# Splitting q and k into three bf16 parts: through PSUM by ScalarE and TensorE in place of VectorE and GpSimd

## The reference

```python
xn = ln(x, ln1_w, ln1_b)                       # after an adaLN norm of x
q = (xn @ q_w + q_b).reshape(B, L, 16, 8)      # 16 heads of 8
k = (xn @ k_w + k_b).reshape(B, L, 16, 8)
v = (xn @ v_w + v_b).reshape(B, L, 16, 8)
attn = softmax(where(causal, q @ k.T * 8 ** -0.5, -inf))
attn_out = (attn @ v) @ o_w + o_b
ssm_out = mamba(xn)                            # conv, silu, a scan over 512 tokens with 16 states
x = x + alpha * attn_out + (1 - alpha) * ssm_out
x = x + gelu(ln(x) @ ffn_w1 + ffn_b1) @ ffn_w2 + ffn_b2
```

## Time and profile before

| what | us |
|---|---|
| median of 3 runs | 1723.49 |
| lowest and highest of them | 1720.03, 1725.16 |
| the profiled execution, its own time | 1718.54 |
| its span from first to last instruction | 1716.3 |
| mean granted TensorE clock, share of full | 0.941 |

### The profile page before, as it was taken

The page is one execution under the profiler, slowest core; times in us unless marked ns, Lnnn a source line. Parts: engine busy times, 40 slices in busy tenths (PEclk is TensorE's granted clock), DMA queues, the critical chain, the costliest instruction groups (busy, mean ns, idle before and its releaser), DMA issues. The chain is left out here.

```text
span 1716.3 us, 22019 instructions
## 1 busy us (share of the span) xinstructions
PE 1425.8 (83%) x7164; PEld 895.0 (52%) x7196; DVE 1336.1 (78%) x2025; ACT 1063.5 (62%) x1776; POOL 848.3 (49%) x866
## 2 busy tenths in 40 slices
PE   4777787887878788797777788799999999968787
PEld 3334444444444344444433655588787777725663
DVE  2359989999898999989961867787677777757856
ACT  2565667586756658576646665687877878722017
POOL 3254768676675777767733312112222222338843
PEclk9878999999999999999989899899999999968889
DMA  3112212222121222212101210011111111000001
GB/s 87 52 48 75 69 59 79 62 70 84 32 88 57 77 70 81 68 42 82 57 1 37 68 53 25 28 38 47 36 47 43 44 46 41 32 0 1 0 1 49
DMA packets 61654, 84.72 MB, mean 49 GB/s; under 512 B 6588, under 2 KB 32038, under 8 KB 61542
## 3 DMA queue, kind: packets, MB, share of 16 engines
q1 hardware_dynamic: 61442, 83.30, 15.5%
q10 hardware_dynamic: 100, 0.03, 0.0%
HBM read 74.38 MB, written 8.78 MB: 48 GB/s over the span
## 5 line engine op out<-in xcount | busy, mean ns | idle before, releaser
L1743 POOL TENSOR_TENSOR dBx<-dtx,Bb 128x512 f32<-128x512 f32 x256 | 320.7, 1275 | 11.4 <-DMA Bb<-b_dram 9.0
L1350 DVE TENSOR_TENSOR hl<-lsq,hh 128x512 fp32r<-128x512 f32 x320 | 260.0, 822 | 84.4 <-ACT hh L1627 76.7
L1317 DVE TENSOR_TENSOR_SCAN hy<-bank,dBx 128x512 f32<-128x512 f32 x256 | 297.9, 1204 | 4.8 <-POOL dBx L1743 4.8
L1035 PE MATMUL bank<-QK 127*128 127x384 bf16 (+6 forms) x992 | 226.1, 309 | 86.6 <-DVE Mx L1301 62.8
L1624 ACT ACTIVATE lsq<-bank,vcol 128x512 f32<-128x512 f32 x320 | 219.5, 693 | 105.2 <-DVE hl L1350 62.7
L1564 ACT ACTIVATE PT<-bank 128x512 f32<-128x512 f32 x320 | 184.5, 595 | 110.9 <-PE bank L1035 66.9
L1762 POOL TENSOR_TENSOR stage<-stage,lrs 128x512 f32<-128x512 f32 x64 | 93.0, 1453 | 309.8 <-DVE lrs L1430 309.8
L1301 DVE TENSOR_REDUCE Mx<-bank 128x1 f32<-128x384 f32 (+3 forms) x352 | 214.0, 627 | 16.4 <-PE bank L1035 16.0
L1035 PE MATMUL bank<-x,we1h 128*128 128x512 f32 x640 | 210.8, 411 | 18.3 <-ACT hh L1627 9.8
L1611 ACT ACTIVATE bank<-dtv,alog 128x512 f32<-128x512 f32 x256 | 171.5, 692 | 80.5 <-DVE hy L1317 79.5
L1723 POOL TENSOR_SCALAR_AFFINE_SELECT PT<-PT 128x256 f32<-128x256 f32 (+1 forms) x320 | 118.4, 378 | 201.4 <-ACT PT L1564 201.0
(11 more groups left out here) (255 smaller groups left out, 2436.8 us busy)
## 6 DMA issues: line engine op xcount, KB each, us to landing
Bb<-b_dram SPq DMA_DIRECT2D x128, 256.0 KB, 3.8
stage<-w_rows SPq DMA_DIRECT2D x64, 256.0 KB, 3.1
parts<-part SPq DMA_DIRECT2D x16, 384.0 KB, 2.8
QK<-parts SPq DMA_DIRECT2D x64, 96.0 KB
QK<-parts SPq DMA_DIRECT2D x64, 64.0 KB
stage<-in_L_ffn_We_dram SPq DMA_DIRECT2D x16, 256.0 KB, 3.5
hy<-in_L_attn_x_dram SPq DMA_DIRECT2D x8, 256.0 KB, 5.7
QK<-parts SPq DMA_DIRECT2D x64, 32.0 KB
```

Of the source, the lines that this page charges most:

```text
L1035: return engine.matmul(o, l, r, start=start, stop=stop, tile_position=pos, skip_group_check=True)
L1317: engine.tensor_tensor_scan(hst[:, 2 * (g % 3) + h, :], bank[4 + h][:], dBx[:, g % 4, h, :], 0.0, ALU.mult, ALU.add).then_inc(sems["dve_sc ...
L1350: engine.tensor_tensor(hl[:, sl, :], full[:, f, :], hh[:, sl, :].bitcast(F32), ALU.subtract).then_inc(sems["dve_hl"], 1)
L1743: engine.tensor_tensor(dBx[:, sl, h], dtx[:, b % 2, h], Bb[:, sl], ALU.mult).then_inc(sems["pool_dbx"], 1)
```

## The change

The split no longer goes through `qf`. TensorE leaves the product in its bank; ScalarE rounds bank plus bias to bf16 part c; TensorE multiplies part c by minus the identity and accumulates it into the same bank; this for c = 0, 1, 2, with two such subtractions. The scale of q goes into its weights, so that the bank holds what is to be split. VectorE and GpSimd have nothing to do in it any more. For this the bank is taken out of the ring until part 2 has been read, ScalarE's first rounding (not VectorE's) waits for the landing of the parts written before, and TensorE's subtractions wait for ScalarE. The buffer `qf` goes, a bf16 matrix `identn` comes.

```diff
-WORK = dict(pe_max=45, pe_sc=30, pe_ht=45, pe_av=200, pe_qk=95, pe_val=95, pe_mrow=45, pe_dn=95, pe_wo=190, pe_bx=350, pe_dbc=180, pe_dt=95,
-            pe_yt=45, pe_so=190, pe_lnc=95, pe_lnv=95, dve_max=62, dve_scan=113, dve_y=40, dve_ha=70, dve_hs=70, dve_yd=70, dve_qk=50,
+WORK = dict(pe_max=45, pe_sc=30, pe_ht=45, pe_av=200, pe_qk=45, pe_val=95, pe_mrow=45, pe_dn=95, pe_wo=190, pe_bx=350, pe_dbc=180, pe_dt=95,
+            pe_yt=45, pe_so=190, pe_lnc=95, pe_lnv=95, dve_max=62, dve_scan=113, dve_y=40, dve_ha=70, dve_hs=70, dve_yd=70, act_qk=62,
...
     def project(b):
         for i in range(2):
             k = take()
-            it = step("qk0", b=b, i=i, bank=k, free=free.get(f"b{k}"), ready=r_n[b], qf=free.get("qf"), part=free.get("part"))
-            it["m"], it["q"], it["h"] = up("pe_qk"), up("act_qf"), up("dve_qk")
-            free[f"b{k}"] = it["q"]
-            h1 = it["h"]
-            yield
-            it = step("qk1", b=b, i=i, h1=h1, part=free.get("part"))
-            it["m1"], it["h2"] = up("dve_qk"), up("dve_qk")
-            h2 = it["h2"]
-            yield
-            it = step("qk2", b=b, i=i, h2=h2, part=free.get("part"), pd=free.get(f"pd{b % 2}"))
-            it["h3"] = free["qf"] = up("pool_qk")
-            it["d"] = free["part"] = r_parts[b] = up(f"parts_{b % 2}", 16)
-            yield
+            ring.remove(k)
+            last = free.get(f"b{k}"), r_n[b]
+            for c in range(3):
+                it = step("qk", b=b, i=i, c=c, bank=k, ready=last, part=free.get("part"), pd=free.get(f"pd{b % 2}"))
+                it["m"] = up("pe_qk")
+                it["x"] = last = up("act_qk")
+                if c == 2:
+                    it["d"] = free["part"] = r_parts[b] = up(f"parts_{b % 2}", 16)
+                    free[f"b{k}"] = last
+                    ring.append(k)
+                yield
...
-                elif kind == "qk0":
-                    q.wait_ge(("pool_set", pool_set["qk3"]), it["free"], it["ready"])
-                    mm(o[:], wqk[:, it["i"], :], nT[:, it["b"], :]).then_inc(sems["pe_qk"], 1)
+                elif kind == "qk":
+                    q.wait_ge(("pool_set", pool_set["idn"]), it["ready"])
+                    if it["c"] == 0:
+                        mm(o[:], wqk[:, it["i"], :], nT[:, it["b"], :], stop=False).then_inc(sems["pe_qk"], 1)
+                    else:
+                        mm(o[:], identn[:], part[:, it["c"] - 1, :], start=False, stop=it["c"] == 2).then_inc(sems["pe_qk"], 1)
...
-                elif kind == "qk0":
-                    q.wait_ge(it["q"], it["part"])
-                    engine.tensor_copy(part[:, 0, :], qf[:]).then_inc(sems["dve_qk"], 1)
-                elif kind == "qk1":
-                    q.wait_ge(it["h1"])
-                    engine.tensor_tensor(qf[:], qf[:], part[:, 0, :], ALU.subtract).then_inc(sems["dve_qk"], 1)
-                    q.wait_ge(it["m1"], it["part"])
-                    engine.tensor_copy(part[:, 1, :], qf[:]).then_inc(sems["dve_qk"], 1)
...
-                elif kind == "qk0":
-                    q.wait_ge(("dve_set", dve_set["qbs"]), it["m"], it["qf"])
-                    engine.activation(qf[:], o[:], ACT.Identity, scale=QS if it["i"] == 0 else 1.0,
-                                      bias=qbs[:, 0:1] if it["i"] == 0 else col("k_b")).then_inc(sems["act_qf"], 1)
+                elif kind == "qk":
+                    q.wait_ge(("dve_set", dve_set["qbs"]), it["m"], it["part"])
+                    engine.activation(part[:, it["c"], :], o[:], ACT.Identity,
+                                      bias=qbs[:, 0:1] if it["i"] == 0 else col("k_b")).then_inc(sems["act_qk"], 1)
...
-                elif kind == "qk2":
-                    q.wait_ge(it["h2"], it["part"])
-                    engine.tensor_tensor(part[:, 2, :], qf[:], part[:, 1, :], ALU.subtract).then_inc(sems["pool_qk"], 1)
...
-                if kind == "qk2":
+                if kind == "qk" and it["c"] == 2:
                     s = it["b"] % 2
-                    q.wait_ge(it["h3"], it["pd"])
+                    q.wait_ge(it["x"], it["pd"])
```

More of the change, by code:

```diff
@@ L898, in build @@
             mrow = small[32:40].bitcast(BF16).rearrange("p (s t) -> p s t", s=2)
-            qf = tmp("qf", [P, T])
+            identn = tmp("identn", [P, P], BF16)
             part = tmp("part", [P, 3, T], BF16)
@@ L986, in on_set @@
             return {name: i + 1 for i, name in enumerate(names.split())}
-        pool_set = on_set("vrow qk0 qk1 qk2 qk3 wo id0 id om cm on ep mask0 mask idb sel0 sel bsum vb0 mr vb qz0 qz1 qz2")
+        pool_set = on_set("vrow qk0 qk1 qk2 qk3 wo id0 id om cm on ep mask0 mask idb idn sel0 sel bsum vb0 mr vb qz0 qz1 qz2")
         dve_set = on_set("row0 row1 sc0 sc1 neg abs sgn2 max sgn gate om1 av2 av3 A qbs")
@@ L1676, in gpsimd_program @@
                 for f in range(2):
-                    engine.tensor_copy(wqk[:, i, 64 * f:64 * f + 64].rearrange("c (q a) -> c q a", a=4),
-                                       wqk0[:, i, 64 * f:64 * f + 64].rearrange("c (a q) -> c q a", a=4)).then_inc(sems["pool_set"], 1)
+                    engine.tensor_scalar(wqk[:, i, 64 * f:64 * f + 64].rearrange("c (q a) -> c q a", a=4),
+                                         wqk0[:, i, 64 * f:64 * f + 64].rearrange("c (a q) -> c q a", a=4), QS if i == 0 else 1.0, None,
+                                         ALU.mult).then_inc(sems["pool_set"], 1)
             engine.memset(wo[:], 0.0).then_inc(sems["pool_set"], 1)
@@ L1693, in gpsimd_program @@
             engine.tensor_copy(identb[:], ident[:]).then_inc(sems["pool_set"], 1)
+            engine.tensor_scalar(identn[:], ident[:], -1.0, None, ALU.mult).then_inc(sems["pool_set"], 1)
             engine.memset(seld[:], 0.0).then_inc(sems["pool_set"], 1)
```

## The result

| what | us |
|---|---|
| before, median of 12 runs beside the change | 1719.55 |
| the change, median of 12 runs (lowest, highest) | 1726.38 (1723.35, 1731.10) |
| ratio, 95% interval | 1.0033 [1.0020, 1.0047], so +5.7 us [+3.4, +8.1] |
| profiled execution of the change: own time, span | 1725.62, 1723.9 |
| its mean granted TensorE clock | 0.928 (before: 0.941) |

The change is slower by about as much as a measurement of this kernel can tell from nothing. The twelve runs of before hold the three of the first table; the ratio leaves out one disturbed run among them (1786.89; experiment J has one of its own, 2062.12, left out likewise). The change's median lies 2.4 us above the forecast of 1724.0 and within its range. Part of that closeness is luck: the forecast was built on the median of three runs, 1723.49, and twelve runs of the same kernel gave 1719.55.

What follows compares the result with a forecast made beforehand. VectorE bounds the mixers overall, but TensorE and ScalarE were taken to set the projections' time. Summed: 5.1 - 4.6 + 6 x 0.0 = +0.5 us, so 1719.0 profiled, 1724.0 as median; range 1712 to 1736.

Steps and rivals of the forecast that it cites:

- Batch 0, +5.1: Serial stretch before the first scan: round trips between TensorE and ScalarE delay the norms, 5.1 us lost, nothing regained.
- Batch 1, -4.6: After the first scan VectorE has no idle time, so its removed split work is all gained: 4.6 us, at worst 2.3.
- The set-up, 0: Before the batches: one more instruction on GpSimd, which is ahead, costs 0.
- Batches 2 to 7, 0.0 each: Six projections: gains and added work end in the scan starting when it did, 0.0 each, bounds -0.9 and +1.2.
- 1.0 us of slack: Last projection: decay ready at about 764.5, scan takes it at 765.55; the additions, +1.0, use this up.
- the first rival: Batches 2 to 7: VectorE's relief counts, 2.9 us gained in each of six, median 1706.6; chance 0.15 with its larger case.
- the 15.9 us of waiting: VectorE's idle time before six roundings in the mixers, waiting for ScalarE; claimed not to be gained.
- 1.3 us at the start: Start of each unit in batches 2 to 7: VectorE's rounding at 724.76 goes; -0.5 counted, -1.3 as bound.
- the second rival: Batches 2 to 7: the held bank leaves four in the ring, VectorE waits for Mx; sum +9, median 1732.4; chance 0.25.
- 0.4 + 1.8: Each of batches 2 to 7: two TensorE subtractions of q, +0.4, and three added ScalarE roundings, +1.8 us.
- a wait of the scan for the decay: Sign: VectorE's scan newly waits 1 to 2 us for ScalarE's decay once per odd unit; without it the first rival holds.
- the number of waits in front of `Mx`: Sign: Mx waiting for TensorE in many more than 25 places would point to the second rival.

Runs made afterwards that it cites:

- J: Kernel before with changed set-up; batches 2 to 7 make only ScalarE's first rounding, bank held out of the ring for three steps; median 1714.53 us, ratio 0.9978.
- B: The change with batch 0 split the old way, batches 1 to 7 the new; median 1722.22 us, ratio 0.9996 to the kernel before.
- C: Kernel before with the changed set-up and batch 1 alone split the new way; median 1719.48 us, ratio 0.9984.
- G: The change with batch 0's split run beside the norms that follow, one step per norm, in bank 3; median 1718.70 us, ratio 0.9993 to the kernel before.
- K: Kernel before with changed set-up, batch 1 alone split the new way, batch 0's old split run beside the norms; median 1715.83 us, ratio 0.9984.
- A: Kernel before with only the change's set-up (scaled wqk, identn), all eight batches split the old way; median 1721.61 us, ratio 0.9995.
- I: Kernel before with changed set-up; batches 2 to 7 make only ScalarE's first rounding, bank given back at once, parts 1 and 2 left out; median 1701.27 us, ratio 0.9898.
- F: Kernel before with VectorE's subtraction and second rounding left out in batches 2 to 7 (part 1 not written); median 1716.70 us, ratio 0.9982.
- D: Kernel before with the changed set-up and batches 2 to 7 alone split the new way; median 1722.03 us, ratio 0.9999.
- E: Kernel before, old split, but each projection bank kept out of the ring until GpSimd's subtraction; median 1734.24 us, ratio 1.0092.
- M: Kernel before with batch 0's split beside the norms, and GpSimd making VectorE's subtraction and second rounding in batches 2 to 7; median 1711.14 us, ratio 0.9938.

## Why the prediction was right, and where it was not

**Batch 0, +5.1: right.** ScalarE's timeline of the changed kernel, and the first of TensorE's two rows for q:

```profile
54.26 0.69 ACT L1546 ACTIVATE part<-bank,qbs 128x512 bf16<-128x512 f32 x1 [3.50 <-PE bank L1033]
55.64 0.69 ACT L1546 ACTIVATE part<-bank,qbs 128x512 bf16<-128x512 f32 x1 [0.70 <-PE bank L1033]
57.03 0.69 ACT L1546 ACTIVATE part<-bank,qbs 128x512 bf16<-128x512 f32 x1 [0.70 <-PE bank L1033]
60.37 0.69 ACT L1546 ACTIVATE part<-bank,vcol 128x512 bf16<-128x512 f32 x1 [2.65 <-DMA parts<-part]
...
63.14 0.69 ACT L1546 ACTIVATE part<-bank,vcol 128x512 bf16<-128x512 f32 x1 [0.70 <-PE bank L1033]
```

```profile
55.00 0.61 PE L1033 MATMUL bank<-part,identn 128*128 128x512 bf16 x1 [0.84 <-ACT part L1546]
```

A round trip takes 1.38 and 1.39 us, in the range of 1.25 to 1.45; the wait for the landing is the 2.65 forecast. From q's first reading to the table load of batch 0's silu it is 49.78 us (54.26 to 104.04) against 44.46 (52.74 to 97.20): +5.3. By the ratios (the change against B) it is +6.4, 3.8 either way. The first scan stands at 123.37, 7.3 us later and not 5; 1.5 of that the first reading of q was late already. The granted clock is 0.50 in this stretch, the 1.2 GHz level, and the product takes 0.61. The 0.1 that the prediction put down for the product's weights does not show (1.38 is 0.69 and 0.61 and 0.08), which keeps the trip below 1.45 on the slow clock. Of the two figures of the Trainium skill (TensorE: Matmul & The Clock Gate, section Single matmul latency) the measured 0.61 is exactly the one for the slow clock.

**Batch 1, -4.6: right at first, then partly taken back.** Measured from the first scan, the scans of the change stand at -2.70, -3.51 and -4.57 behind the three places of the earlier trace rows (the scans of 121.60, 135.15 and 146.19 before): VectorE's rows were worth their whole length. The prediction stopped there. At the scan of 155.58 it is -3.87, and -3.63 at 163.30, since the freed VectorE meets TensorE in its convolutions. And in B, C and G more went. The convolution in the changed kernel and in B, with the row of VectorE's wait in B:

```profile
146.88 3.69 PE L1033 MATMUL bank<-nT,wtap 128*128 128x512 f32 x8 [1.61 <-DVE Mx L1294]
```

```profile
142.04 6.68 PE L1057 MATMUL bank<-nT,wtap 128*128 128x512 f32 x8 [1.61 <-DVE Mx L1329]
...
149.03 0.69 DVE L1329 TENSOR_REDUCE Mx<-bank 128x1 f32<-128x512 f32 x1 [2.64 <-PE bank L1057]
```

The same eight products took 3.69 and 6.68 us (4.76 in the trace before, 5.41 in C, 6.69 in G). In B the granted clock was 0.50 from 136 to 146 us; TensorE had waited for VectorE there for 2.28 us at 137.05 and for 1.61 us just ahead of the convolution. The change had nearly the same waits (1.89 us at 141.89, then 1.61) and was back at 1.00 when its convolution began; why B was not stays open. At the scan of 163.30 B had kept 0.6 of its 4.6 us, C 1.9 and G 0.6, the change 3.6 and K 3.6. The prediction let a gain come back only through a decay that is held up; it came back through TensorE.

**The set-up, 0: not refuted.** Most traces say 1 to 3 us at the first reading of q, K's and the medians nothing (A). The step named the one instruction added and overlooked that the four scaled copies stand ahead of ident, for which TensorE waits.

**Batches 2 to 7, 0.0 each: the sum right by luck, the steps wrong.** The prediction let five of VectorE's six instructions lie "inside the time that TensorE and ScalarE set", and put the scan of 765.55 behind a decay with 1.0 us of slack. I and F show otherwise. VectorE's relief is worth 2.8 us in each of the six (16.7/6, known to 0.6), where the first rival had 2.9; only the 15.9 us of waiting stayed, as the prediction said. Where k's part of it comes through can be read in the last projection. On TensorE before, the scores ahead of dt's second product waited for an `Mx` that stood behind VectorE's work on k:

```profile
758.53 0.39 PE L1035 MATMUL bank<-QK 128*128 128x384 bf16 x2 [0.51 <-DVE Mx L1301]
```

ScalarE then waited 0.46 us for that product. In F neither waits, and there stand:

```profile
755.89 1.29 ACT L1614 ACTIVATE bank<-dtv,alog 128x512 f32<-128x512 f32 x2
...
756.69 2.33 DVE L1320 TENSOR_TENSOR_SCAN hy<-bank,dBx 128x512 f32<-128x512 f32 x2
```

The scans ahead of VectorE's work on k come 7.38 us earlier than before, this decay 7.95 (it stood at 763.84) and this scan 8.86. So the decay itself moved by 0.57, and the other 0.9 of the 1.48 is the slack that the prediction had kept for the additions.

The prediction's own list holds most of this. Its 1.3 us at the start, the 0.7 of waits that are swallowed and the slack of 1.0 make 3.0 for each batch, close to the 2.8 measured; its words about the five instructions, and the argument against the first rival, leave it out. Wrong in size were the two prices. The held bank takes 13.8 us, 2.3 for each batch; the main sum had let it take 0.8 of the 1.3 at the start of a unit, and the second rival had +9 in all. The roundings and subtractions take 3.6, 0.6 for each (1.1 by the scans), where the sum had 0.4 + 1.8. The one was too small by about as much as the other was too large. In the last projection of the change the roundings show. ScalarE:

```profile
746.63 0.69 ACT L1570 ACTIVATE xc<-bank,vcol 128x512 f32<-128x512 f32 x1 [5.33 <-PE bank L1033]
747.21 0.68 ACT L1546 ACTIVATE part<-bank,qbs 128x512 bf16<-128x512 f32 x1
...
760.16 0.69 ACT L1546 ACTIVATE part<-bank,vcol 128x512 bf16<-128x512 f32 x1
...
769.42 0.67 ACT L1546 ACTIVATE part<-bank,vcol 128x512 bf16<-128x512 f32 x1
...
770.47 1.30 ACT L1604 ACTIVATE bank<-dtv,alog 128x512 f32<-128x512 f32 x2
```

and VectorE, with the pause in front of bc and the wait for the decay:

```profile
757.39 0.22 DVE L1305 COPY bc<-bank 128x64 f32<-128x64 f32 x1 [2.38 <-PE bank L1033]
...
771.61 2.34 DVE L1310 TENSOR_TENSOR_SCAN hy<-bank,dBx 128x512 f32<-128x512 f32 x2 [1.06 <-ACT bank L1604]
```

All three roundings stand where the prediction put them, and the scan waits 1.06 us. That is the longest of the six, which make 4.6 in all, so most lie below the forecast of 1 to 2. Without the additions (I) such a wait is 0.3 at most. The Trainium skill's rule that speaks against the move (VectorE: DVE Perf Modes, section The perf-mode tier table) agrees with this as far as it goes: it covers the rounding that VectorE gave up, 0.43 us at its quickest, and the 0.69 on ScalarE is read from the trace. But the price of the move was mostly in the bank that is held, of which the rule says nothing.

So the rivals of relief and of the held bank were both true, with -16.7 and +13.8 us, and given as alternatives with 0.15 and 0.25. What made the forecast hold is that they cancel. The check that the prediction named, a wait of the scan for the decay, came true and did not tell its account from this one; its other sign, the number of waits in front of `Mx`, pointed to the held bank.

**The total.** By the ratios: set-up -0.9 (A, within its error), batch 0 +6.4 (the change against B), batches 2 to 7 +0.7 (D against A), batch 1 -1.9 (C against A): +4.3, where +5.7 was measured. Each of these four terms is known to 2.5 to 4 us either way. Of the 5.2 us between the forecast difference of +0.5 and the measured one, the largest single part by these terms is batch 1, 2.7 us less gain than forecast; batch 0 has 1.3.

## What to carry to other kernels

An engine that waits for a late result does not show where the time is set if that result waits in its turn for this engine: leave the work out once and look, before calling it covered. A PSUM bank kept through a round trip has a price of its own, which can be as large as the work it saves; measure it by holding the bank with nothing else changed. And an engine with room that needs no bank (GpSimd here) may be the better place for the work.

## What the runs showed of the hardware

- One bank fewer in a ring of five, for more than half of each odd unit, cost 15.8 us of 1719 (E), nearly three times what the change as a whole costs.
- The freed time of one engine can be lost where TensorE's granted clock is low: the same convolution took 3.69 us in the change (granted clock 1.00) and 6.68 in B (0.50 until 146 us). F's runs fell into 1707 us at a mean granted clock of 0.934 and 1715 to 1722 at about 0.92, with one program.
- On GpSimd a rounding of 128x512 from float32 to bf16 took 0.61 us in M, against 0.69 for the same rounding from PSUM on ScalarE, and 1.16 for the subtraction, against 0.68 to 1.38 on VectorE.
